# Joining an expert stage to the stage ahead of it: one program part for all five engines, with the second unit's rows, the weight loads and the last two units reordered

## What is computed

```python
x = x + attn(_layernorm(x))                    # state-space block
h = _rmsnorm(_layernorm(x)) ; flat = h.reshape(T, 512)     # T = 2048
scores = softmax(flat @ router_w.T)            # 32 experts
topk_w, topk_ids = top_k(scores, 4) ; topk_w /= sum(topk_w)
# for each of the 4 experts e of a token:
#   g, u = split(flat @ w1[e]) ; ys = (silu(g) * u) @ w2[e]
routed = sum over the 4 of ys * topk_w
shared = silu(flat @ sg) * (flat @ su) @ sd
x = x + residual + routed + shared
```

## Time and profile before

| | |
|---|---|
| median of 3 runs | 1617.28 us (1613.62 to 1618.94) |
| the profiled execution, its own time | 1620.9 us |
| its span, first to last instruction | 1618.9 us |
| mean granted TensorE clock | 0.963 of full |
| TensorE busy | 1449.8 us (90% of the span) |
| VectorE / ScalarE / GpSimd busy | 1308.3 / 741.5 / 1077.6 us |
| DMA, software queue (GpSimd's) | 37.32 MB, 11.1% of the 16 engines' span |
| DMA, hardware queue (SyncE's) | 138.59 MB, 24.8% |

### The profile page before, as it was taken

The page is one execution under the profiler, slowest core; times in us unless marked ns, Lnnn a source line. Parts: engine busy times, 40 slices in busy tenths (PEclk is TensorE's granted clock), DMA queues, the critical chain, the costliest instruction groups (busy, mean ns, idle before and its releaser), DMA issues. The chain is left out here.

```text
span 1618.9 us, 14732 instructions
## 1 busy us (share of the span) xinstructions
PE 1449.8 (90%) x4412; PEld 725.0 (45%) x4413; DVE 1308.3 (81%) x1931; ACT 741.5 (46%) x1160; POOL 1077.6 (67%) x545
## 2 busy tenths in 40 slices
PE   6578998889998889998798878899998999999996
PEld 3233443334443334443343323444445766667774
DVE  4599999999999999999999997355636777777772
ACT  4566665776656776657566664421000111111111
POOL 0199898999887999989999997230011455555453
PEclk9889999899999999999899999999999999999998
DMA  4540112410113411103310004021412888888895
GB/s 131 221 174 9 42 48 101 179 40 30 35 47 108 171 41 36 35 15 126 129 36 21 28 1 156 20 104 33 182 54 64 225 237 225 218 239 223 259 260 68
DMA packets 63823, 176.86 MB, mean 109 GB/s; under 512 B 10304, under 2 KB 15168, under 8 KB 55040
## 3 DMA queue, kind: packets, MB, share of 16 engines
q1 hardware_dynamic: 48128, 138.59, 24.8%
q0 software_dynamic: 15616, 37.32, 11.1%
HBM read 142.98 MB, written 32.85 MB: 109 GB/s over the span
## 5 line engine op out<-in xcount | busy, mean ns | idle before, releaser
L1342 POOL TENSOR_TENSOR h<-h,c_rep 128x2048 f32<-128x2048 f32 x128 | 579.3, 4530 | 31.2 <-DVE h L945 26.1
L1542 PE MATMUL bank<-h,ident 128*128 128x512 f32 x916 | 449.3, 634 | 93.0 <-POOL h L1342 74.2
L717 ACT ACTIVATE bank<-delta,a_neg 128x512 f32<-128x512 f32 x512 | 335.8, 682 | 178.9 <-DVE h L945 178.1
L1542 PEld LDWEIGHTS bank<-h,ident 128*128 128x128 f32 x916 | 180.6, 202 | 335.9 <-issue 210.9
L945 DVE TENSOR_TENSOR_SCAN h<-bank,state,h 128x512 f32<-128x512 f32 x256 | 306.0, 1260 | 0.5 <-ACT bank L717 0.5
L945 DVE TENSOR_TENSOR_SCAN h<-bank,h 128x512 f32<-128x512 f32 x256 | 290.7, 1199 | 2.8 <-ACT bank L717 2.6
L171 DVE STREAM_TRANSPOSE xT<-xg 32x256 f32<-32x256 f32 (+1 forms) x592 | 247.3, 418 | 56.0 <-DMA xg<-flat,slot_token 48.3
L935 DVE TENSOR_TENSOR h<-bank,b_rep 128x2048 f32<-128x2048 f32 (+1 forms) x105 | 227.5, 2184 | 35.7 <-ACT bank L708 24.2
L1703 POOL DMA_INDIRECT out<-y,slot_token x64 | 101.8, 1590 | 110.1 <-DMA out<-y,slot_token 65.2
L1329 POOL TENSOR_TENSOR h<-du,b_rep 128x2048 f32<-128x2048 f32 (+1 forms) x32 | 125.4, 3920 | 11.5 <-PE bank L1542 11.5
L1787 ACT ACTIVATE y<-y_ps,share 128x512 f32<-128x512 f32 x69 | 47.4, 687 | 185.3 <-PE y_ps L1935 152.3
(11 more groups left out here) (238 smaller groups left out, 1530.0 us busy)
## 6 DMA issues: line engine op xcount, KB each, us to landing
w_ring<-in_w SPq DMA_DIRECT2D x32, 1024.0 KB, 5.3
b_rep<-bcd SPq DMA_DIRECT2D x16, 1024.0 KB, 6.9
c_rep<-bcd SPq DMA_DIRECT2D x16, 1024.0 KB, 5.0
w_ring<-in_w SPq DMA_DIRECT2D x32, 512.0 KB, 7.4
w_in<-in_w_in_x SPq DMA_DIRECT2D x32, 256.0 KB, 2.6
w_res<-in_w_in_res SPq DMA_DIRECT2D x32, 256.0 KB, 2.6
xa<-in_x SPq DMA_DIRECT2D x20, 256.0 KB, 3.0
xb<-in_x SPq DMA_DIRECT2D x16, 256.0 KB, 3.0
```

What stands on the lines that cost most here:

```text
L717: eng.activation(da[j][:], delta[:, g % 2], ACT.Exp, scale=a_neg[:, col:col + 1])\
L1342: ins = eng.tensor_tensor(h[:, q], h[:, q], c_rep[:, Q * q:Q * q + Q, :], ALU.mult)
L1542: ins = eng.matmul(y_ps[:], c.ident[:], h[:, q, j, :], start=False, stop=(q == NQ - 1 and j == Q - 1))
```

## The change

- The bodies of the experts' engine programs become functions that are called at the end of `front`'s programs. There is one block, and no meeting of engines in the middle. GpSimd gets a wait on `upper_listed` of its own. PSUM banks 0 to 5 are reused by name.
- VectorE transposes the rows of units 0 and 1 at the end of `front`, both ahead of `add(12)` to `add(15)`. `rows_turned(1)` goes from the experts' part.
- SyncE loads `w1` of a place as soon as the last unit of place `p - 4` is through `up` (`up_done`), and `w2` after its `down`, as before.
- The last two units: TensorE runs `down(35)`, `gate(36)`, `up(36)`, `down(36)`; ScalarE scales unit 35 ahead of the silu of unit 36.

```diff
@@ front
+        c.bank, c.upper_listed = bank, F["upper_listed"]
+        feed_experts, gather_experts, silu_experts, mult_experts, run_experts = experts(nc, c, dram, ctx)
...
                 eng.wait_ge(F["upper_listed"], 32)
+                feed_experts(eng)
...
                         base_row(2 * u + 1)
+                silu_experts(eng)
...
-                for v in (0, 1):
-                    eng.wait_ge(c.gathered[v], 16)
-                c.turned(eng, 0, 2)
+                for u in (0, 1):
+                    for v in (0, 1):
+                        eng.wait_ge(c.gathered[2 * u + v], 16)
+                    c.turned(eng, u, 2).then_inc(c.xT_ready, 1)
                 for i in range(UNITS - HC, UNITS):
                     add(i)
+                mult_experts(eng)
...
+                gather_experts(eng)
...
+                run_experts(eng)
@@ experts (indentation apart)
-        g_ps = [ctx.enter_context(nc.psum_tensor(f"g_ps{i}", [P, 512], F32)) for i in range(2)]
...
+    g_ps, u_ps, y_ps = (c.bank[0], c.bank[2]), (c.bank[1], c.bank[3]), (c.bank[4], c.bank[5])
...
+    def unit_of(n):
+        return next(u for u in range(NU) if n in slots_of(u))
...
-                    eng.wait_ge(S["y_done"], last_slot(place - RING) + 1)
+            eng.wait_ge(S["up_done"], unit_of(last_slot(place - RING)) + 1)
                     eng.dma_start(c.w1r[:, u], ...).then_inc(c.w_landed[u], 16)
+            eng.wait_ge(S["y_done"], last_slot(place - RING) + 1)
                     eng.dma_start(c.w2r[:, u], ...).then_inc(c.w_landed[u], 16)
...
-                        after(eng, S["xT_ready"], old)
+                eng.wait_ge(S["xT_ready"], old + 1)
...
                 eng.wait_ge(c.base_stored, 16 * TT)
+        eng.wait_ge(c.upper_listed, 32)
...
                 for u in range(NU):
-                    if u + 1 < NU:
+            if u < NU - 2:
                         silu_gate(u + 1)
...
                         weighted(n)
+            if u == NU - 2:
+                silu_gate(u + 1)
...
-                rows_landed(eng, 0)
-                shares_of(0)
-                rows_turned(1)
+        for u in range(EARLY // 2):
+            rows_landed(eng, u)
+            shares_of(u)
                 mult(0)
...
-                    after(eng, S["xT_ready"], u)
+            eng.wait_ge(S["xT_ready"], u + 1)
...
-                for u in range(NU):
-                    if u + 1 < NU:
+        for u in range(NU - 2):
                         gate(u + 1)
...
                     down(u)
+        down(NU - 2)
+        gate(NU - 1)
+        up(NU - 1)
+        down(NU - 1)
```

654 lines of the change are left out of this document (322 added, 332 removed).

## The result

The changed kernel takes 1623.04 us (median of 9 executions, 1619.39 to 1626.29). The kernel before, executed beside it, takes 1616.37 us (9, 1608.5 to 1619.92). The ratio is 1.0039, 95% interval 1.0020 to 1.0057: slower by 0.39%, some 6 us. This ratio, like those of the experiments, is taken over the executions measured side by side and is not the plain quotient of the two medians, which is 1.0041 here. The profiled execution took 1623.04 us with a span of 1621.0 us, 2.1 us more than the profiled one of before.

A forecast was written before the change was run, and what follows sets the result against it. The bound was taken as the first `y` plus one serial chain of scatter issues and landings. Median 1617.28 + 2.85 (first `y`) + 0.8 (median) - 1.4 (chain) = 1619.5 us, 0.14% slower; range 1615 to 1624.

The forecast's parts named there:

- What bounds the kernel: Expert stage: the end is the first `y` plus one serial chain of scatter issues and landings; TensorE is dragged along.
- The second set ahead of the adds: End of front: VectorE's second 16 transpositions delay `add(12)`, `dn(14)` and `dn(15)` by 7.17 us; TensorE idles 7.8 us.
- the meeting and second unit's rows: Start of experts: waits of 1.82 and 2.02 us and slow matmuls go, 6.0 us; with the stall, first `y` 1.15 later.
- The clock: TensorE behind the 7.8 us idle before `dn(14)`: half speed loses 1.7 us, from a range of 1.66 to 2.85.
- Against the median: Going from profiled execution to median: some executions lack the 1.69 us clock loss, so half of it, 0.8 us, is added.
- The chain behind it, the early `w1`: Scatter chain: one MB less lies on it, the last load is 0.5 MB instead of 1.5; 1.4 us gained (0 to 2.7).
- In most units nothing moves in time: SyncE's weight loads: though they look reordered, 1.5 MB still goes out at the same moment as before in most units.
- The price itself: Scatter chain: one load of 1.5 MB costs a period 10.42 - 8.37 = 2.05 us.
- The split burst: Once a group, 0.5 MB stays and 1 MB goes about 3.5 us later; counted as zero, the least certain term.
- the slower rival: The moved MB meets the first pair of scatters in the later four groups, 7.2 us: 1626.7 us; chance 0.17.
- The last two units: Units 35 and 36: one ready some 7 us earlier, the other about 1 later, hidden by the chain; zero below 6 us.
- The faster rival: TensorE leads the expert stage: row waits save 6.0 us, the last units' order 3.0, giving 1610.5 us; chance 0.17.

The follow-up runs named there:

- half of `up`: Changed kernel with the up product of two-slot units over half of its contraction, 8 instead of 16 matmuls a unit: 1625.21 us, ratio 1.0035 to the kernel before.
- 8 filler calls: Changed kernel with 8 needless matmul calls in TensorE's idle time just ahead of `dn(14)`: 1621.91 us, ratio 1.0011 to the kernel before.
- adds between the sets with the rest as before: Changed kernel with `add(12)`, `add(13)` between the two transposition sets, the others behind; loads and last units' order as before: 1613.04 us, ratio 0.9966 to the kernel before.
- relief by a quarter of `w1`: Changed kernel with each reload of `w1` bringing only its first quarter, 0.25 MB instead of 1 MB: 1609.55 us, ratio 0.9926 to the kernel before.

## Why the prediction was right in its mechanism and short in its size

**What bounds the kernel** was read rightly: the first `y` plus one serial chain, TensorE dragged along. With TensorE's work cut by 55 us the chain stays at 358.8 us; with the DMA engines relieved it falls to 345.5 us; and in eleven profiles with full loads and full matmuls it stays between 355.0 and 358.9 us, whatever the border does. The ratios follow the stage step roughly: -6.0 us gave -6.6 and -5.5 us (ratio times 1617), -4.7 gave -3.1, +1.2 gave +1.8, +3.3 gave +3.4, +3.5 gave +6.3, +4.1 gave +4.7, +6.9 gave +7.9. Two kernels stand off the line, the early-`w1` undone (+4.0 gave +0.6) and half of `up` (0.0 gave +5.7). With intervals of 3 us to either side the first may be chance. By the quotients of the medians the early-`w1` undone stands off less (+2.0) and the 8 filler calls more (+3.9).

**The second set ahead of the adds, and the meeting and second unit's rows**: right. The stall is 7.82 us for a forecast 7.8, and the border without the clock is +1.21 us (8 filler calls) for a forecast +1.15.

**The clock**: right in kind, too small. I took 1.7 us, near the lower rows; the seven profiles show 2.1 to 2.9 us, on average 2.5, which is the upper half of the range from the earlier trace rows. By the stage step the first `y` came 3.5 and 4.1 us later, not 2.85. The losses behind 2.0 and 2.6 us of idle time were 1.69 and 1.66 us, those behind 3.40 us were 1.66 and 2.85 us. Two losses that far apart behind the same idle time say that its length alone does not fix the loss; with 7.8 us of it there was no reason to take the lowest value of the range and not its middle, 2.25.

**Against the median**: a step that failed. I put part of the profiled execution's surplus down to a clock loss that other executions would lack. The second profile of the kernel before has the same loss to a hundredth, and is faster by its chain, 355.5 us. Two of two profiles have the loss, so there was no ground to add anything; this +0.8 went in the right direction by luck.

**The chain behind it, the early `w1`**: forecast -1.4 us, and -1.36 between the two first profiles, but that agreement is luck. Over all profiles with full loads and matmuls the chain is 356.0 us on average with the early `w1` (six: 357.5, 355.7, 355.4, 355.0, 356.1, 356.1) and 356.8 without (five: 358.9, 355.5, 356.2, 357.4, 356.1), a difference of 0.8 us with a spread of 3 in either group; 2.5 us of the last one come from the order of the last units. The periods show what such a total is made of:

- The MB issued ahead of the chain saves nothing: the period of the first pair falls from 11.0 to 8.3 us, and the next grows from 15.4 to 18.4, so that the third batch starts 25.8 to 27.6 us after the first scatter with the early `w1` and 25.9 to 26.7 without.
- The period of the last load falls from between 10.3 and 11.3 us to between 7.8 and 8.2, by 2.6 us on average: here the term of 1.4 was too small.
- "In most units nothing moves in time" is the other step that failed. The six periods from unit 25's pair to unit 31's take 64.8 to 66.9 us in the six profiles with the early `w1`, and 62.3 to 63.4 us in four of the five without (57.1 in the fifth, adds between the sets with the rest as before, where the pairs of units 25 to 30 started 3 to 6 us after their `y` instead of 10 to 16). With unit 31's own period it is 73.1 to 75.1 us against 72.9 to 74.0: what the last load saves has been lost just before, although one MB less is issued there. It shows already in the kernel that differs from the changed one by the loads alone, 62.5 against 65.6 and 64.8 us.

The loads do move in these units. Before, SyncE issues `w1` and then `w2` 0.5 us apart; in the changed kernel `w2` goes first and `w1` 1.1 us behind it (SyncE's queue before, then after):

```profile
1558.13 0.33 SPq L1670 DMA_DIRECT2D w_ring<-in_w  x1
1558.65 0.33 SPq L1671 DMA_DIRECT2D w_ring<-in_w  x1
```

```profile
1561.94 0.33 SPq L1679 DMA_DIRECT2D w_ring<-in_w  x1
1563.03 0.34 SPq L1677 DMA_DIRECT2D w_ring<-in_w  x1
```

Whether the order of the two, the distance between them or where they fall beside the scatters makes the periods longer, no run tells apart. The price itself, 2.05 us for a load, was not a clean one either: the period of 8.37 us from 1443.13 to 1451.50 that I took for one without a load on the landing had one issued in it (SyncE's queue, before):

```profile
1448.69 0.33 SPq L1670 DMA_DIRECT2D w_ring<-in_w  x1
```

So the saving at the end is shown, and so is its loss ahead of it; a net gain in time is not. Undoing the part gave a total that is no worse.

**The split burst**: zero, as counted, and the slower rival is not there. In the first such group the period from the first pair to the second falls from 10.8 to 8.1 us and the one ahead of it grows from 12.5 to 14.7 (means over the same eleven profiles): what the bytes take from one period (2.7 us) they nearly give back to the one ahead (2.3 us). By these periods the moved MB meets the scatters ahead of the pair, not the pair; by unit 25 the two groups of profiles are level to within 1 us on average. The Trainium skill, DMA: Bandwidth & Descriptors, section Issuing engines are not separate DMA queues, says that transfers of all engines run on the same 16 DMA engines. The relief by a quarter of `w1` agrees with it (chain 345.5 us at a DMA share of 0.71); the time of 1626.7 us that I had hung on it did not come: the pairs that the rival priced got faster, and the scatters ahead of them slower.

**The last two units**: zero, as forecast, but with less to spare. I had put the point at 6 us. Before, unit 35's pair started 4.7 and 4.5 us after its `y`, and with the adds between the sets and the old order once at 0.27 us. The faster rival, TensorE leading, is wrong for both kernels, yet it names the next bound: as an estimate from these distances, with the old order it sets in once the chain is some 3 to 5 us shorter at that point.

**The sum.** The border measured +3.5 and +4.1 us for +2.85, and the chain nothing sure for -1.4. With the false +0.8 left out, the terms give 1617.28 + 3.8 + (-0.8 to 0) = 1620.3 to 1621.1 us, ratio 1.0019 to 1.0024. Both measurements hold that within their intervals, or nearly (1.0020 to 1.0057 and 1.0008 to 1.0050), but their middles lie 1 to 3 us above it. That rest is not explained. The 1623.04 us lie within the stated range of 1615 to 1624, near its end; that the ratio came out above the 0.3% up to which I had called it no change, 1.0039 where 1.0014 was forecast, is a matter of 3 to 4 us, and the interval reaches below that bound.

## What to carry to other kernels

Before a block of work is moved ahead of small instructions that free another engine's buffers, ask who waits for those: here 7.2 us of transpositions ahead of 0.7 us adds and the half clock behind them cost more than the meeting of all engines and the wait for rows that the change removed, and the same block one step later cost nothing. Where a stage is one serial chain of issues and landings, cost a change as the shift of the chain's start plus the change of its length, check each by its own row in more than one profile, and test slot by slot whether work waits for its own input; the releaser that a view names may be a pass that ended there by accident. Compare two profiles of the same kernel before a difference of 3 us is given a cause.

## What the runs showed of the hardware

- Behind 7.8 us of idle time TensorE lost 2.1 to 2.9 us in its next 7.1 us of work, at a granted clock of 0.50 for the first 4.6 us in one of seven such profiles and for 5.8 us in another; with needless matmuls in that time and 0.94 us idle it lost none. The loss varied by 0.7 us between executions whose instructions at the border are the same.
- A call of an fp32 matmul with 512 columns became two instructions: 8 calls were 16 instructions and 7.03 us, 16 calls 32 and 13.90 us.
- What a weight load costs a chain of scatters depends on when it is issued. In the first group with a split burst, 1 MB issued one set of matmuls later shortened one period by 2.7 us and lengthened the one ahead of it by 2.3 us. In units 25 to 31, `w2` first and `w1` 1.1 us behind it gave six periods of 64.8 to 66.9 us, `w1` first and `w2` 0.5 us behind it 62.3 to 63.4 us (four of five profiles). A mechanism for either is not shown.
- Two executions of the kernel before, alike at the border to a hundredth of a microsecond, differed by 3.4 us in their chains of landings (358.90 and 355.52 us).
